# Expert stage of a graph-and-experts layer: tiles of 256 tokens in place of 128, the first product with its output units on partitions, its matrix fetched again for each tile

## The reference, cut to what matters

```python
D, H, E = 256, 1024, 8; TOP_K = 2
xf = layernorm(x)                                # 6250 x 256
top_w, top_i = top_k(xf @ Wg + bg, 2); top_w = softmax(top_w)
w_dense = sum(one_hot(top_i, 8) * top_w[..., None], axis=1)
for e in range(8):
    h = gelu(xf @ W1[e] + b1[e], approximate=False)          # 256 -> 1024
    out = out + w_dense[:, e:e+1] * (h @ W2[e] + b2[e])      # 1024 -> 256
result = x + out
```

## Time and profile before

| | |
|---|---|
| median of 3 runs | 5801.03 us (5793.69 to 5807.15) |
| profiled execution, its time | 5790.27 us |
| its span | 5788.6 us |
| TensorE, VectorE, ScalarE, GpSimd busy | 76%, 56%, 49%, 61% of the span |
| mean granted TensorE clock | 0.855 of full speed |
| stages ahead of the expert stage | up to about 4900 us |

### The profile page before, as it was taken

The page is one execution under the profiler, slowest core; times in us unless marked ns, Lnnn a source line. Parts: engine busy times, 40 slices in busy tenths (PEclk is TensorE's granted clock), DMA queues, the critical chain, the costliest instruction groups (busy, mean ns, idle before and its releaser), DMA issues. The chain is left out here.

```text
span 5788.6 us, 85756 instructions
## 1 busy us (share of the span) xinstructions
PE 4371.0 (76%) x20831; PEld 3233.2 (56%) x20831; DVE 3235.0 (56%) x8923; ACT 2815.7 (49%) x8615; POOL 3552.6 (61%) x3708
## 2 busy tenths in 40 slices
PE   7588888888888888656666666665665546999998
PEld 4466666666666666544444444444444434666666
DVE  5477777777677777754545454544444456222232
ACT  2576767677676766434444444433333342222222
POOL 0577777777777777017777777777777741233333
PEclk9798999999899899877788778777777766999999
DMA  5888888888888888235555555555666553411111
GB/s 184 244 242 247 240 240 242 240 245 241 240 246 238 242 239 246 85 118 141 144 143 142 139 144 143 140 136 156 164 166 170 158 149 105 142 49 51 51 51 39
DMA packets 689524, 975.33 MB, mean 168 GB/s; under 512 B 390410, under 2 KB 482408, under 8 KB 688798
## 3 DMA queue, kind: packets, MB, share of 16 engines
q0 software_dynamic: 228304, 716.77, 43.3%
q1 hardware_dynamic: 460190, 252.19, 15.8%
q10 hardware_dynamic: 560, 1.05, 0.1%
HBM read 899.62 MB, written 64.56 MB: 167 GB/s over the span
## 5 line engine op out<-in xcount | busy, mean ns | idle before, releaser
L859 POOL DMA_INDIRECT walk_ring<-s_h,walk_index x3320 | 3194.8, 962 | 1423.8 <-issue 928.3
L1020 PE MATMUL walk_pM<-walk_ring,walk_hit 128*128 128x262 f32 (+1 forms) x9960 | 2761.5, 430 | 13.0 <-ACT walk_ring L884 6.8
L1020 PEld LDWEIGHTS walk_pM<-walk_ring,walk_hit 128*128 128x128 f32 x9960 | 2026.4, 211 | 418.6 <-issue 73.2
L884 ACT ACTIVATE walk_ring<-walk_ring 128x128 f32<-128x128 f32 (+1 forms) x6640 | 2134.4, 414 | 5.4
L1250 DVE TENSOR_TENSOR acc<-walk_pM,acc 128x520 f32 (+1 forms) x1494 | 832.8, 557 | 584.0 <-PE walk_pM L1020 563.2
L874 ACT ACTIVATE walk_ring<-walk_gap 128x40 f32<-128x40 f32 (+1 forms) x249 | 54.1, 258 | 1898.6 <-DVE walk_gap L1212 1898.6
L924 PE MATMUL walk_pC<-all_ident,walk_best 128*84 128x128 f32 (+1 forms) x166 | 61.7, 372 | 1063.7 <-DVE walk_best L1168 986.0
L924 PEld LDWEIGHTS walk_pC<-all_ident,walk_best 128*84 128x84 f32 (+1 forms) x166 | 20.6, 124 | 1126.2 <-issue 1126.2
L1217 DVE TENSOR_TENSOR walk_hit<-walk_pK,walk_meta 128x512 f32<-128x512 f32 x830 | 560.7, 676 | 11.9
L2021 ACT ACTIVATE expert_hT<-expert_pG,expert_b 128x128 f32<-128x128 f32 x840 | 228.2, 382 | 615.7 <-PE expert_pG L2091 615.6
L1168 DVE TENSOR_TENSOR walk_best<-walk_ring,walk_dt 128x40 f32<-128x40 f32 (+1 forms) x249 | 47.2, 217 | 859.8 <-DMA walk_ring<-s_h,walk_index 859.8
(11 more groups left out here) (316 smaller groups left out, 4032.0 us busy)
## 6 DMA issues: line engine op xcount, KB each, us to landing
walk_hitT<-s_places SPq DMA_DIRECT2D x166, 640.0 KB
walk_ring<-s_h,walk_index POOLq DMA_INDIRECT x3320
expert_w<-in_fw_dram SPq DMA_DIRECT2D x16, 1024.0 KB, 6.5
walk_goal<-walk_target SPq DMA_DIRECT2D x830, 6.0 KB
walk_goal<-walk_target SPq DMA_DIRECT2D x830, 1.5 KB
walk_xk<-s_xT SPq DMA_DIRECT2D x98, 128.0 KB, 2.8
walk_resets<-s_resets SPq DMA_DIRECT2D x415, 20.0 KB
s_h<-first_h_out SPq DMA_DIRECT2D x7, 1056.0 KB, 4.3
```

The lines of the kernel that those rows point to most:

```text
L859: pool.indirect_dma_start(ring[:, r % RS, t, :], None, table, bass.IndirectOffsetOnAxis(ap=index[:, r % TS, t:t + 1], axis=0)).then_inc(ro ...
L884: last = nc.scalar.activation(row, row, ACT.Copy, scale=ring[:, r % RS, t, at + FH:at + FH + 1])
L1020: last = nc.tensor.matmul(pM[:, b, a, 0:WIDE], hit[:, (r * CGROUPS + g) % HBUF, t % GROUP, :], ring[:, r % RS, t, a * HALF_ROW:a * HALF_RO ...
```

## The change

What it does:

- A tile has 256 slots (`XT`), made of two halves h of 128. `TT = (12500 + 8 * 255) // 256 = 56` tiles, `TH = 112` halves. The table of token numbers has 112 columns, each expert's slots are rounded up to 256, and `expert` has 56 entries. The indirect DMAs still move 128 rows each, so there are 112 of each kind.
- `up` takes w1 as the stationary operand and streams 256 tokens past it: 8 groups of 128 units, 2 matmuls of 256 columns each, into four PSUM banks, two groups to a bank. The units come out on partitions. `turn`, pG, `copy_pre` and `pre` are gone. Gelu reads pH bank by bank as each is done, 8 instructions of 256 columns. hT is double.
- `down` runs for each half: 8 matmuls of 256 columns, as before.
- w1 is no longer kept for all experts. `load_up(t)` reads the tile's expert into a register of SP and fetches its 1 MB into slot t % 4. From tile 4 on it waits for the end of `up(t-4)`.
- w2 of all experts stays. Behind the first turned tile SP now issues `load_up(1)` to `load_up(3)` with `load_down(1)` to `load_down(3)`, then `load_down(4)` to `load_down(7)`, ten transfers of 1 MB with no wait between them, and only then reports which w2 have landed.
- POOL gathers the totals of both halves at the head of a tile, when both halves of the tile before are stored, then for each half gathers tokens and scatters totals. Tokens are gathered ten halves ahead into a ring of twelve.

```diff
-TT = (2 * N + NEXP * (P - 1)) // P
+XT = 2 * P
+TT = (2 * N + NEXP * (XT - 1)) // XT
+TH = 2 * TT
...
-                    last = nc.tensor.matmul(pI[:, 0:TT], place_of[:, n % PICKS, :], token_of[:, n % PICKS, :],
+                    last = nc.tensor.matmul(pI[:, 0:TH], place_of[:, n % PICKS, :], token_of[:, n % PICKS, :],
...
+                def load_up(t):
+                    e = sp.value_load(k["expert"][0:1, t:t + 1], min_val=0, max_val=NEXP - 1)
+                    if t >= WS:
+                        sp.wait_ge(up_done, (t - WS + 1) * BANKS)
+                    sp.dma_start(w1[:, t % WS, :, :], d["fw1"].rearrange("e (k p) h -> p e k h", p=P)[:, bass.ds(e, 1), :, :]...).then_inc(up_in[t % WS], 16)
...
+                load_up(0)
+                load_down(0)
+                sp.dma_start(b2[:, :, :], d["fb2"].partition_broadcast(P)).then_inc(bias_in, 16)
+                sp.wait_ge(x_turned, 1)
+                for t in range(1, WS):
+                    load_up(t)
+                    load_down(t)
+                for e in range(WS, NEXP):
+                    load_down(e)
+                for e in range(WS):
+                    report_down(e)
+                load_up(WS)
+                for e in range(WS, NEXP):
+                    report_down(e)
+                for t in range(WS + 1, TT):
+                    load_up(t)
...
+                for h in range(SX - 2):
+                    gather_tokens(h)
                 for t in range(TT):
                     gather_totals(t)
+                    for q in range(2):
+                        h = 2 * t + q
+                        if h + SX - 2 < TH:
+                            gather_tokens(h + SX - 2)
+                        scatter_totals(h)
...
+                    for j in range(BANKS):
+                        act.wait_ge(up_done, t * BANKS + j + 1)
+                        for c in range(j * HB, (j + 1) * HB):
+                            nc.scalar.activation(hT[:, t % 2, c, :], pH[:, j, c % HB, :], ACT.Gelu, bias=b1[:, e, c:c + 1]).then_inc(h_ready, 1)
...
+                for t in range(TT):
+                    if t + 2 < TT:
+                        copy_tokens(t + 2)
+                    e = dve.value_load(...)
+                    for h in (2 * t, 2 * t + 1):
+                        take_out(h, e)
+                        add_total(h, e)
...
                 def up(t):
+                    pe.wait_ge(up_in[t % WS], 16 * (t // WS + 1))
+                    pe.wait_ge(xT_ready, t + 1)
+                    for j in range(BANKS):
+                        if t >= 1:
+                            pe.wait_ge(h_ready, (t - 1) * HC + (j + 1) * HB)
+                        for c in range(j * HB, (j + 1) * HB):
+                            for kk in range(DK):
+                                last = nc.tensor.matmul(pH[:, j, c % HB, :], w1[:, t % WS, kk, c * P:(c + 1) * P], xT[:, t % 2, kk, :],
+                                                        start=(kk == 0), stop=(kk == DK - 1))
+                        last.then_inc(up_done, 1)
...
                 def down(t):
                     e = pe.value_load(...)
                     pe.wait_ge(experts_in, e + 1)
+                    for q in range(2):
...
+                turn_tokens(0)
+                up(0)
+                turn_tokens(1)
                 for t in range(TT):
                     if t + 1 < TT:
+                        up(t + 1)
                     if t + 2 < TT:
                         turn_tokens(t + 2)
+                    down(t)
```

More of the change, by code:

```diff
@@ L2012, in _ @@
+                for j in range(4):
+                    pool.wait_ge(total_stored[j], 16 * len(range(j, TH, 4)))
             @block.scalar
@@ new lines, in take_out, with add_total @@
+                def take_out(h, e):
+                    dve.wait_ge(down_done, h + 1)
+                    nc.vector.tensor_tensor(out[:, h % 2, :], pO[:, h % 2, 0:D], b2[:, e, :], ALU.add).then_inc(out_ready, 1)
+                def add_total(h, e):
+                    dve.wait_ge(out_ready, h + 1)
+                    dve.wait_ge(total_in[h % 4], 16 * (h // 4 + 1))
+                    nc.vector.scalar_tensor_tensor(out=total[:, h % 4, :], in0=out[:, h % 2, :], scalar=xin[:, h % SX, bass.ds(e + D, 1)],
+                                                   in1=total[:, h % 4, :], op0=ALU.mult, op1=ALU.add).then_inc(total_ready, 1)
@@ L2076, in up, with down @@
+                def down(t):
                     e = pe.value_load(k["expert"][0:1, t:t + 1], min_val=0, max_val=NEXP - 1)
                     pe.wait_ge(experts_in, e + 1)
-                    pe.wait_ge(xT_ready, t + 1)
-                    if t >= 1:
-                        pe.wait_ge(pre_ready, t)
-                    for a in range(2):
-                        for kk in range(DK):
-                            last = nc.tensor.matmul(pH[:, a, :], xT[:, t % 2, kk, :], w1[:, e, kk, a * 512:(a + 1) * 512],
-                                                    start=(kk == 0), stop=(kk == 1))
@@ L2085, in up @@
-                    last.then_inc(up_done, 1)
-                    return e
-                def turn(t):
-                    pe.wait_ge(pre_ready, t + 1)
-                    for c in range(HC):
-                        last = nc.tensor.transpose(pG[:, c, :], pre[:, c * P:(c + 1) * P], k["ident"][:, :])
-                    last.then_inc(pre_turned, 1)
-                def down(t, e):
-                    if t >= 2:
-                        pe.wait_ge(out_ready, t - 1)
-                    for c in range(HC):
-                        pe.wait_ge(h_ready, t * HC + c + 1)
-                        last = nc.tensor.matmul(pO[:, t % 2, 0:D], hT[:, c, :], w2[:, e, c, :], start=(c == 0), stop=(c == HC - 1))
-                    last.then_inc(down_done, 1)
@@ L2102, in _ @@
-                expert = [None] * TT
+                    for q in range(2):
+                        if t >= 1:
+                            pe.wait_ge(out_ready, 2 * (t - 1) + q + 1)
+                        for c in range(HC):
+                            if q == 0:
+                                pe.wait_ge(h_ready, t * HC + c + 1)
+                            last = nc.tensor.matmul(pO[:, q, 0:D], hT[:, t % 2, c, q * P:(q + 1) * P], w2[:, e, c, :], start=(c == 0), stop=(c == HC - 1))
+                        last.then_inc(down_done, 1)
```

150 lines of the change are left out of this document (53 added, 97 removed).

## The result

The changed kernel takes 5746.79 us in the median of five runs (5740.29 to 5764.99), the kernel before 5798.67 us (5793.69 to 5807.15) in five on the same chip. The ratio is 0.9922, 95% interval 0.9904 to 0.9939: 51.9 us faster, where 55.8 were forecast. By the interval the gain lies between 35 and 56 us.

What follows compares the result with a forecast made beforehand. Bound before: two loops of almost one length, TensorE's 7.99 and memory's 8.05 us a tile of 128. Terms sum to 817.4 us where 873.2 stood, 55.8 less: 5801.03 becomes 5745 us, range 5731 to 5768.

Steps and rivals of the forecast that it cites:

- TensorE's tile: TensorE's steady work: 14.26 us a tile of 256, 56 tiles 798.6 us against 839, gain 40.
- The memory loop of before: Scatter, gather of totals, add, scatter: 8.05 us a tile of 128 against TensorE's 7.99, no slack.
- gather to add: Memory loop: from a totals gather's start to the add it releases, 4.01 us, read in the tail.
- The fetch: Steady part: w1's 1.05 MB a tile meets gathers but fits 3.6 us of slack; 1 us in all, bounds 0 and 25.
- rival 1: Steady part: the fetch makes the memory loop the bound, 17.4 us a tile, 5924 us in all; chance 4%.
- last scatter to first gather: Memory loop at 256 tokens: a tile's last scatter releases the next tile's first totals gather after 2.71 us.
- Start: Stage's beginning: first `up` 1 us later, its slow clock 2.4, copy before `up(1)` 1.2, first `down` delayed 6.
- SP's hold at the ten transfers: Start: SP, held issuing ten transfers, reports w2 late and the first `down` waits; 6 us, bounds 0 and 14.
- The first `up`: Start: it ran 5.94 us for 3.60 before; that loss of 2.4 us stays.
- the copy ahead of `up(1)`: Start: `turn_tokens(1)` and the copy stand exposed before the second `up`, 0.69 + 0.5 = 1.2 us.
- Tail: End: 2.1 us from last product to last scatter, then 4.76 to the end of the span; 6.9 us.
- The weight-load rival: `up`: weight loads of 0.190 us show for each of 32 records, 6.1 us a tile, 6085 in all; chance 1%.

Runs made afterwards that it cites:

- e5: Changed kernel with 16 transposes of the identity into a spare bank added to each tile of 256: 6826.32 us, kernel before beside it 6790.40.
- e11: Kernel before with seven more padding tiles of 128, 112 in place of 105: 5856.37 us, kernel before beside it 5795.53.
- e1: Kernel before with the 8 transposes of each tile left out, so values differ from the reference: 5716.55 us, kernel before beside it 5802.06.
- e3: Kernel before, tiles still 128, with the first product's units on partitions, w1 from fixed slots, no transposes or copy: 5731.52 us, kernel before 5802.06.
- e7: Changed kernel with a second 1 MB transfer a tile into a buffer nobody reads: 6734.88 us, kernel before beside it 6790.40.
- e9: Against the kernel before: tiles of 128, units on partitions, w1 fetched per tile, early w2 report, late b2 wait: 6850.44 us, kernel before 6790.40.
- e12: Same kernel as e9, run again on the other chip: 5861.83 us, kernel before beside it 5795.53.
- e4: Changed kernel with SP reporting expert 0's w2 after issuing w1 of tiles 1 and 2, before the other eight transfers: 5746.56 us.
- e2: e1 with totals gathered two tiles ahead from a table nothing writes, against the kernel before: 5690.83 us, kernel before beside it 5802.06.
- e13: Same kernel as e3, run again: 5740.19 us, kernel before beside it 5795.53.
- e8: e4 with a tile's two halves sharing one semaphore per kind of indirect DMA, ten for twenty: 6731.86 us, kernel before beside it 6790.40.
- e10: Changed kernel with early w2 report, shared semaphores and b2 awaited only before the first take_out: 5737.52 us, kernel before beside it 5795.53.

## Why the prediction was right, and where it was not

The forecast was 5745 us and the median is 5746.79. That the two lie within 2 us is in part luck: the interval of the gain is 20 us wide, and one term of the sum was off by 8.9 us. What the runs support is the mechanism of the steady part, which makes up most of the gain.

- *TensorE's tile.* Forecast 14.26 us, measured 14.25; the `up` record is 0.216 as borrowed from `down`. 40 us of gain, as said. e5 shows that each record counts, e11 that seven tiles of padding cost nearly their full price (54 us for 56).
- *The memory loop of before.* This step failed. The prediction called it 8.05 us, without slack, and said that a shorter TensorE tile at 128 tokens would bring nothing. e1 brought 85 us. The mis-sized term is gather to add: 4.01 us was read in the tail, and in the steady part it is 3.09 (e1) or 2.96 (median of e3). Nor is a delay of that loop never made up: the late gather at 5234.00 cost nothing one tile later. The prediction even had the sign of it, 3.97 fitting in a tile of 7.99, and took the loop for equal all the same; that row shows only an upper bound, since the add there waited for VectorE's own copy. The trace of the kernel before had the price itself, 2.91 us in the one tile of 600 us in which an add waited for its gather. The forecast didn't hang on it, because at 256 tokens either price leaves slack.
- *The fetch.* Forecast free with 3.6 us of slack, 1 us in all. Measured 0. e7 shows room for twice as much, and e9 and e12 show rival 1 at 128 tokens. The slack itself wasn't measured, since in the steady part no add waited for a gather: gather to add is shorter by 0.9 us than said, but last scatter to first gather took 3.2 us (5311.38 to 5314.60) for the 2.71 of the sum.
- *Start.* SP's hold at the ten transfers was forecast at 6 us and measured at 7.1 (4.00 idle, 3.1 of slow clock); e4 took it away. The first `up`, at a granted clock of 0.55 from 4935 to 4940 us, cost 2.3 (2.4 forecast), the copy ahead of `up(1)` 1.0 (1.2). The stage's start came no later than before relative to SP's first issue (14.60 us for 14.90), where 1 us was added. From the first `up` to the end of the last product the sum says 798.2 + 2.4 + 1.2 + 6 + 1 = 808.8 us, and the trace 5743.5 - 4935.04 = 808.5.
- *Tail.* Forecast 6.9 us, measured 5759.3 - 5743.5 = 15.8. Of the 8.9 us more, 2.8 are a late last scatter: the last two `down` stand back to back, and the add waits 4.71 us for its gather. The other 6.2 come behind the last scatter, 10.95 for 4.76, nearly all in the drain of GpSimd. The tail is the term of the sum that was off, and it is why the stage gained 49.3 us where the sum has 56.5 for it (the 55.8, and the 0.7 that it adds ahead of the stage). A start 1.3 us shorter than forecast pays back a little. What lengthens the drain stays open.
- *The weight-load rival* had 1% at 256 columns; by e3 it is false down to 128 columns. So the answer was right and the test for it was not: the prediction held the length of a load's record (0.190) against the distance of the matmuls (0.216), and in e3 the same load hides under 0.112. The kernel before has such a case too, in `turn`: loads of 0.141 us in the median, 0.109 apart. The Trainium skill, "Perfetto Trace Analysis", Optimizing Tensor Performance, speaks for larger matmuls. The traces don't bear it out between 512 and 256 columns, 0.84 ns a column and record each; 128 columns cost 0.87, 4% more.

## What to carry to other kernels

A price for a loop has to come from where the loop really waits, and whether it sets the pace is told by the waits in the steady part: a gap in which something else was the last to finish gives only an upper bound, and a tail has other prices than the steady part. Where a memory loop runs beside TensorE, doubling the tile doubles the time for its fixed latencies, and that slack can pay for traffic: a fetch of 1 MB for each tile of 128 cost 121 us of the stage at 166 GB/s, and with tiles of 256 even 203 GB/s cost nothing. Where executions differ by 20 us in stages that weren't touched, compare the touched stage from its own first event.

## What the runs showed of the hardware

- Streams of float32 weight load and matmul pass at 0.112 us a record with 128 streamed columns, though each load's record is 0.19 us long (e3).
- The last drain of GpSimd took 2.17 us (before, e1, e2, e3, e9, e12, e13), 3.89 (e11), 7.16 (e8, e10) or 8.30 (after, e4, e5, e7), always the same value for the same kernel. Ten semaphores for twenty took 1.14 us off (e4 to e8), seven more tiles with 21 more indirect DMAs added 1.72 (before to e11), and together these are not half of the 6.13 between before and after. What sets the rest stays open.
- Two chips ran the same edge walks about 1000 us apart, with the expert stage alike where its tiles are 256 (838.2 and 836.8; 831.9 and 830.7 us). At 128 tokens with a fetch the stage took 932.5 us on one and 955.9 on the other (e9, e12).
